# Own places for the first and last row, another lead order on GpSimd and ScalarE, and all eight rows as straight code

## What is computed

```python
h = x + xattn(layernorm(x), ctx, ctx)        # softmax(q k^T / 4) v, then Wo, bo
h1 = einsum('gmh,goh->gmo', layernorm(h), W1) + b1   # g = row, 8 of them, no nonlinearity
out = h + einsum('gmo,gho->gmh', h1, W2) + b2
```

## Time and profile before

| | us |
|---|---|
| median of three runs | 559.8 |
| lowest and highest of them | 554.53, 560.4 |
| the profiled execution | 550.82 |
| its span, first to last instruction | 548.7 |
| PE busy in the span | 529.4 (96%) |
| DVE, ACT, POOL busy | 456.7, 387.0, 278.7 |

### The profile page before, as it was taken

How to read it: one execution, slowest core, us unless ns; L and a number is a source line. 1 busy time by engine, 2 the same in 40 slices (tenths; PEclk the granted TensorE clock), 3 DMA queues, 4 the chain that set the end, 5 groups by cost and what they waited for, 6 DMA issues and landing times.

```text
span 548.7 us, 13740 instructions
## 1 busy us (share of the span) xinstructions
PE 529.4 (96%) x4515; PEld 350.3 (64%) x4515; DVE 456.7 (83%) x841; ACT 387.0 (71%) x704; POOL 278.7 (51%) x320
## 2 busy tenths in 40 slices
PE   8999999999999999999988999999999999989987
PEld 7876674665666667666565666666666667544466
DVE  5896858899989999899877999899889999878234
ACT  7225657877887787777875777776888787667831
POOL 7136417751876159732865149741876156413131
PEclk9986999999999999999998999999999999999999
DMA  7666265535763466555652565544653366130201
GB/s 251 137 161 204 70 182 140 155 89 131 210 162 105 118 186 184 149 146 154 170 157 62 132 184 161 173 111 131 188 159 91 71 184 164 42 78 2 92 9 38
DMA packets 46742, 73.12 MB, mean 133 GB/s; under 512 B 12162, under 2 KB 22730, under 8 KB 46666
## 3 DMA queue, kind: packets, MB, share of 16 engines
q1 hardware_dynamic: 46666, 72.18, 48.0%
HBM read 41.99 MB, written 4.47 MB: 85 GB/s over the span
## 4 chain that ended last, share of the span: by engine, by line
PE 64%; DVE 10%; issue 7%; ACT 6%; SPq 5%; DMA 5%; POOL 3%; DVEq 0%; POOLq 0%; ACTq 0%
PE pv L589 17%; PE st L575 13%; PE nat L564 8%; PE misc L769 7%; PE misc L650 7%; PE misc L640 7%; DVE neg_max L1150 5%; ACT probs L969 4%; SPq L401 3%; ACT normed L1016 2%; DMA qs<-max_hi 2%; DMA x_in<-x 2%; DVE stats L1160 1%; PE st L551 1%; DVE y L1228 1%
## 5 line engine op out<-in xcount | busy, mean ns | idle before, releaser
L969 ACT ACTIVATE probs<-st 128x512 f32<-128x512 f32 x502 | 285.8, 599 | 127.6 <-PE st L575 120.9
L1150 DVE TENSOR_REDUCE neg_max<-nat 128x1 f32<-128x512 f32 x505 | 330.4, 682 | 52.3 <-PE nat L564 48.6
L564 PE MATMUL nat<-ks,qs 63*128 63x512 f32 x505 | 224.9, 468 | 2.5 <-DVE neg_max L1150 1.3
L575 PE MATMUL st<-qs,ks 64*128 64x512 f32 x502 | 217.9, 465 | 7.0 <-issue 2.9
L575 PEld LDWEIGHTS st<-qs,ks 64*128 64x128 f32 x502 | 90.2, 187 | 92.3 <-ACT probs L969 61.8
L589 PE MATMUL pv<-probs,vs 128*32 128x512 f32 x1024 | 133.1, 609 | 1.2 <-ACT probs L969 1.2
L564 PEld LDWEIGHTS nat<-ks,qs 63*128 63x128 f32 x505 | 91.5, 187 | 10.6 <-DVE neg_max L1150 5.3
L769 PE MATMUL misc<-w_in 64*128 64x256 f32 x512 | 74.0, 378 | 0.0
L1391 POOL TENSOR_SCALAR var_eps<-mean_var 128x4 f32<-128x4 f32 x16 | 3.6, 227 | 117.0 <-DVE mean_var L1166 109.4
L769 PEld LDWEIGHTS misc<-w_in 64*128 64x128 f32 x512 | 53.6, 188 | 5.8 <-issue 1.7
L589 PEld LDWEIGHTS pv<-probs,vs 128*32 128x32 f32 x1024 | 22.7, 108 | 45.6 <-issue 34.4
(11 more groups left out here) (223 smaller groups left out, 1049.9 us busy)
## 6 DMA issues: line engine op xcount, KB each, us to landing
ks<-hi SPq DMA_DIRECT2D x64, 128.0 KB, 2.5
qs<-hi SPq DMA_DIRECT2D x64, 128.0 KB, 2.6
w_in<-w SPq DMA_DIRECT2D x16, 512.0 KB
w_in<-w2T SPq DMA_DIRECT2D x16, 512.0 KB
x_in<-x SPq DMA_DIRECT2D x8, 512.0 KB, 4.2
ctx_in<-ctxT SPq DMA_DIRECT2D x8, 512.0 KB, 4.4
ks<-lo SPq DMA_DIRECT2D x32, 128.0 KB, 2.5
qs<-lo SPq DMA_DIRECT2D x32, 128.0 KB, 2.6
```

Of the source, the lines that this page charges most:

```text
L564: mm((nat_of(n) if bank is None else bank)[:, :], qs[own, 2 * g + jj, c * P:(c + 1) * P], ks[own, 2 * g + jj, :], start=True, stop=True).t ...
L575: mm(st_of(u, prep)[:, :], ks[rows(jp), 2 * g + jj, kc * P:(kc + 1) * P], qs[rows(jp), 2 * g + jj, :], start=True, stop=True).then_inc(st_ ...
L969: act.activation(probs[kc % PROBS][:, j, :], st_of(u, prep)[:, :], ACT.Exp).then_inc(exp_done, 1)
L1150: dve.tensor_reduce(neg_max[:, g % 2, at:at + 1], (nat_of(n) if bank is None else bank)[:, :], AX.X, ALU.max, negate=True).then_inc(max_do ...
```

## The change

`turns` becomes a plain loop of the program that writes the kernel, so each engine has eight turns of straight code; `wait_apart` becomes `wait`, and the register values and the `passed` semaphores go. The tables move into a class `Steady` with the values of before, with `First` for row 0 and `Final` for row 7 beside it, which replace some of them; `places(b)` picks one, and steps with places over 64 go by the table of the row that they belong to.

```diff
+            for b in range(B):
+                turn(b, b % 2, b > 0, b < LAST, b < LAST - 1)
-            turn(0, 0, False, True, True)
-            turn(1, 1, True, True, True)
-            with eng.Fori(1, B // 2 - 1) as pair:
-                turn(2 * pair, 0, True, True, True)
-                turn(2 * pair + 1, 1, True, True, True)
-            turn(B - 2, 0, True, True, False)
-            turn(B - 1, 1, True, False, False)
...
+class First(Steady):
+    CHAIN_UNITS = ((0, 0, 0, 0, 0, 0), (3, 3, 5, 6, 6, 7), (9, 9, 9, 9, 10, 10), (10, 11, 11, 11, 11, 11), (13, 13, 13, 13, 13, 14), (17, 17, 17, 26, 31, 32), (32, 33, 34, 35, 35, 35), (37, 37, 38, 38, 38, 39), (41, 42, 42, 42, 43, 43))
+    W21_UNITS = (48, 48, 49, 50, 51, 52, 55, 58, 60, 60, 66, 66, 67, 67, 68, 68)
+    MAXT_UNITS = ((56, 56), (7, 8), (22, 26), (44, 44))
+    PV_UNITS = (4, 10, 15, 22, 24, 33, 36, 40, 44, 45, 47, 54, 57, 61, 62, 64)
+    HI_AT = (9, 9, 11, 15)
+    STATS_AT = (13, 14, 27, 27)
...
+class Final(Steady):
+    CHAIN_UNITS = ((0, 0, 0, 0, 0, 0), (2, 2, 6, 6, 6, 6), (6, 6, 9, 12, 12, 13), (13, 16, 17, 17, 19, 19), (19, 19, 20, 21, 22, 22), (23, 24, 25, 26, 27, 27), (28, 28, 28, 28, 29, 29), (30, 34, 34, 34, 36, 36), (36, 36, 40, 44, 46, 46))
+    YT_UNITS = (37, 37, 37, 37, 37, 37, 37, 37)
+    Z_UNITS = (43, 44, 44, 48, 55, 55, 55, 55)
+    MAXT_UNITS = ((34, 60), (11, 11), (24, 25), (37, 39))
+    PV_UNITS = (8, 13, 15, 17, 30, 31, 34, 36, 39, 46, 50, 53, 58, 61, 65, 66)
+    MASK_AT = (50, 63)
+    MAX_AT = (39, 12, 27, 43)
+    OUT_AT = (61, 62)
...
-FIRST_W21_UNITS = (21, 23, 23, 25, 25, 25, 25, 26, 27, 27, 27, 27, 27, 27, 27, 27)
+FIRST_W21_UNITS = (15, 16, 17, 19, 20, 20, 26, 26, 28, 28, 28, 29, 29, 30, 31, 31)
-FIRST_X_SPLIT_AT = 6
+FIRST_X_SPLIT_AT = 0
+FIRST_WO_AT = 9
-LAST_ST = 44
+LAST_ST = 40
```

SyncE, in turn 0:

```diff
+                if not post:
+                    load_ffn(0, 0)
+                    load_ffn(0, 1)
+                    load_bias(0)
                 if load:
                     load_x(b + 2)
```

```diff
-                    if not post and u < FIRST_WARM:
-                        wait(pe, v_ready, 2)
-                        warm_half(0, WARM_BANKS)
-                        warm_half(1, WARM_BANKS)
```

ScalarE: `ctx_split(1)` moves from unit 1 to just ahead of the turns, `x_split(1)` to unit 0; the activation into `odd_sum` at unit 57 of the last row gets a wait for `even_out`. VectorE: `w_rest(WO)` moves from ahead of the turns into unit 9 of row 0. GpSimd's lead:

```diff
             inverse_root(0, 1)
+            x_norm(1)
+            ctx_rest(1)
             pool.wait_ge(const_in, CONSTS)
-            v_stack(0, 0)
-            v_stack(0, 1)
-            x_norm(1)
-            v_stack(0, 2)
-            v_stack(0, 3)
-            ctx_rest(1)
+            for g in range(QUADS):
+                v_stack(0, g)
             x_rest(1)
```

More of the change, by code:

```diff
@@ L793, in jobs @@
             def jobs(b, odd, u, post, prep, load):
-                for n, at in enumerate(W21_UNITS):
+                here, prior = places(b), places(b - 1)
+                for n, at in enumerate(prior.W21_UNITS):
                     if post and at == UNITS + u:
                         w21_step(b, n, prep)
-                for t, at in enumerate(MAXT_UNITS[1]):
+                for t, at in enumerate(here.MAXT_UNITS[1]):
                     if at == u:
@@ L812, in jobs @@
                         w21_step(0, n, True)
-                for t, at in enumerate(MAXT_UNITS[2]):
+                for t, at in enumerate(here.MAXT_UNITS[2]):
                     if at == u:
@@ L817, in jobs @@
                                 wait(pe, lo_ready, 4 * (b + 1) + 4)
-                            wait_apart(pe, max_done, UNITS * b + 48)
+                            wait(pe, max_done, UNITS * b + 48)
                         maxT_half(b, 2, t)
-                for n, at in enumerate(YT_UNITS):
+                for n, at in enumerate(here.YT_UNITS):
                     if post and at == u:
@@ L826, in jobs @@
                                 wait(pe, v_ready, 2 * (b + 1) + 1)
-                            wait_apart(pe, norm_ready[1], 4 * b)
+                            wait(pe, norm_ready[1], 4 * b)
                         yT_step(b - 1, n)
-                for t, at in enumerate(MAXT_UNITS[3]):
+                for t, at in enumerate(here.MAXT_UNITS[3]):
                     if at == u:
@@ L835, in jobs @@
                                 wait(pe, y_ready, 2 * b - 1)
-                            wait_apart(pe, max_done, UNITS * b + 64)
+                            wait(pe, max_done, UNITS * b + 64)
                         maxT_half(b, 3, t)
-                for n, at in enumerate(Z_UNITS):
+                for n, at in enumerate(here.Z_UNITS):
                     if post and at == u:
@@ L843, in jobs @@
                         z_step(b - 1, 1 - odd, n)
-                for n, at in enumerate(W21_UNITS):
+                for n, at in enumerate(here.W21_UNITS):
                     if prep and at == u:
@@ L848, in jobs @@
                         w21_step(b + 1, n, load)
-                for t, at in enumerate(MAXT_UNITS[0]):
+                for t, at in enumerate(here.MAXT_UNITS[0]):
                     if prep and at == u:
@@ L854, in jobs @@
                                 wait(pe, out_ready, 2 * b)
-                            wait_apart(pe, max_done, UNITS * (b + 1) + 16)
+                            wait(pe, max_done, UNITS * (b + 1) + 16)
                         maxT_half(b + 1, 0, t)
             def turn(b, odd, post, prep, load):
+                here, prior = places(b), places(b - 1)
                 for u in range(UNITS):
@@ L1163, in aggregate @@
                 wait(dve, stat_done[which], 4 * b + 4)
-                wait_apart(dve, rstd_ready[which], b)
+                wait(dve, rstd_ready[which], b)
                 for c in range(C):
@@ L1242, in turn @@
             def turn(b, odd, post, prep, load):
+                here = places(b)
                 for u in range(UNITS):
@@ L1245, in turn @@
                         row_max(row, n)
-                    for c, at in enumerate(STATS_AT):
+                    if not post and u == FIRST_WO_AT:
+                        w_rest(WO)
+                    for c, at in enumerate(here.STATS_AT):
                         if load and at == u:
```

254 lines of the change are left out of this document (133 added, 121 removed).

## The result

| | before, us | after, us |
|---|---|---|
| median of four runs each, on one chip | 557.72 | 537.66 |
| lowest and highest | 554.53, 560.40 | 536.48, 537.96 |
| profiled execution | 550.82 | 537.72 |
| its span | 548.7 | 535.9 |

The ratio is 0.9639, with a 95% interval of 0.9575 to 0.9702. The two profiled executions are only 13.1 apart. So there are two things to read: where the 13.1 lie, and why the medians are a further 7 us apart.

What follows compares the result with a forecast made beforehand. PE was taken to bound a row, at about 60 us. Straight code 6.2, row 0 with the lead 4.0 and the last row 1.5 sum to 11.7 us off 559.8: median 548.1, range 538 to 556.

Steps and rivals of the forecast that it cites:

- I take the savings off the median as they stand: Whole kernel: savings summed against the profiled 550.8 us are subtracted from the timed median 559.8, 9.0 above it.
- straight code: Rows 2 to 5: without the loop's jump back and register instructions, 6.2 us saved, between 4.2 and 7.5.
- the last row: Row 7: new places close PE's holes and pair work better, 1.5 us saved, between -1 and 4.
- half of the rest: Loop rows: besides the jump's 4.86 us, half of the 2.67 by which the other three stretches exceed row 1.
- rival E: Rows 2 to 5: straight code makes PE's fetch late, 4.4 to 4.9 us each, up to 576; chance 0.03.
- The lead: Ahead of row 0: POOL's and ACT's new order readies ctx 8.3 us and xT 7.9 us earlier.
- Row 0's term: Row 0: earlier ctx and xT and a shorter low clock save 4.0 us, with ends 1.0 and 6.1.
- rival D: Row 0: the clock never falls, so the row gives 6.1 us and the median is 546.0; chance 0.05.
- my -1: Last row: pair 0's mask, 0.7 us of ACT, moves from unit 29 to 50, where ACT is busy: -1.
- rival B: Last row: y comes late for the tail, the row loses 3.5 us, median 553.1; chance 0.08.
- Rival C: Whole kernel: only the loop's jump counts and the tables are worth nothing, median 554.9; chance 0.08.
- Rival A: Row 0: the clock stays low through its start, so the row gives 1.0 us, median 551.1; chance 0.14.

Runs made afterwards that it cites:

- repeated run of before: The kernel before, timed and profiled again with no edit: 556.39 us, ratio 1.0035; its profile fell on an execution of 560.66 us.
- the 34 runs: Those of 45 unedited runs of the kernel before, on three chips, that the ratios use: median 557.0 us, 550.80 to 562.03.
- lead-only kernel: Changed kernel with row 0's tables, warm-up pairs and SP's order as before; POOL's and ACT's lead order and W_O's split as changed: 537.35 us, ratio 0.9678.
- second-half kernel: Changed kernel with the last row's places as before up to unit 35, new from unit 36 on, LAST_ST 40: 542.43 us, ratio 0.9755.

## Why the prediction was wrong in size, and what it had right

**The step that failed** is the one that I passed over in a sentence: "I take the savings off the median as they stand". It treats the 9.0 us between the profiled execution and the median as a constant that the change can't touch. The repeated run of before shows what it can be: falls of the clock in the last row, 20.5 us in that execution, which the one profile I had did not contain. That profile's low time was 17.6 us (clock 0.984), where the 34 runs have 28.7; at 0.38 us each that is 4.2 of the 6.2 us between 550.8 and 557.0. The new places take most of that low time away, the last row's above all. By the same slope, as an estimate, the change from 28.7 to 8.3 us is worth 7.8 us of the median's 20.1, and 12.3 are left at equal clock. Forecast were 11.7, of which 3.0 (4.0 less 1.0) stood for a shorter low clock in row 0. I had seen this in the range, with 4 us, and gave it no rival of its own.

By terms, in the medians and taken out one at a time, straight code is worth 7.9 to 8.3 us (taken at 6.2), row 0 and the lead 2.2 (taken at 4.0), and the last row 9.4 (taken at 1.5). That makes 19.5 to 19.9 of the 20.1. The term that was mis-sized by most is the last row's, and its error alone is nearly the whole miss.

**Straight code**, taken at 6.2 between 4.2 and 7.5, gave 7.7 between the profiles, 6.9 when added alone and 7.9 to 8.3 when taken out. The mechanism was right: PE's hole at the jump, 2.9 us, is gone, and the low clock behind it with it. Mis-sized was "half of the rest": the 2.67 us by which the loop's other stretches exceed row 1 was no scatter. With the loop back they are 60.2 to 60.6 again, in straight code 59.5, at full clock both times. The difference between the stretches showed it, and the argument that the register instructions are beside running matmuls was no reason to halve it. That the register instructions are what makes the loop's rows longer is not shown apart from the increments.

**Late fetch in straight code** (rival E) did not come: four rows within 0.03 us of each other. The Trainium skill (Runtime: NRT & Kernel Launch, Instruction fetch mechanics) has straight code fetched ahead in sequence, and this trace agrees.

**The lead** came as worked out: ctx_lo at 37.0 (36.3 forecast), xT_lo at 40.9 (40.6), PE's wait for ctx 0.43 and 0.63 us in the two profiles of the changed kernel and not 1.1. In row 0 the clock was back at 49.72, later than the 48 that I had set as a sign, and in the second profile at 44.83 (44.6 forecast), where the first `odd_sum` stands at 79.45 (79.5 forecast). That last hit is luck in part: I had counted the work up to unit 37, and `First` has the copy behind unit 40. **Row 0's term** of 4.0 was nevertheless too high: 2.2 came. The step that failed in it is the marker. I read the gain at unit 37, by 83.40. Between the profiles the way from the first unit to that copy shrank by 3.5 us (48.8 to 45.4), but the way from there to the second copy grew by 2.2 (24.51 to 26.68), because `First` puts most of the v products behind unit 37. The reading "so it is slow there and not idle" was not enough either: where the clock was full, PE waited for ctx_lo instead and came to the second copy no sooner, so the late ctx was the limit there and not the clock. The lead-only kernel shows that the tables on the whole bring nothing beyond the earlier ctx. (In the sum, a clock that never falls makes 77.9 by its own figures and not 77.3, so rival D was worth 5.5 and not 6.1.)

**The last row**, taken at 1.5 between -1 and 4, gave 5.0 at full clock and 7.9 to 9.4 in the medians, outside its own range by either. I counted PE's idle time in it, and under 1 us for better pairing, as all that could be won, and took 1.5. The idle time did go (2.8 of the 4.25), but PE's busy time fell as well, by 2.1 in the three stretches, and in the medians the clock came on top. The mask in the fuller stretch of ACT, my -1, is not seen: that stretch is 2.3 us shorter.

**y in time** (rival B): forecast with a margin of 1.9, measured with 1.4, so it did not decide. **Rival C**, only the jump, is excluded by 537.66. **Rival A and rival D** stood for the clock in row 0. The changed kernel lies between them, 6.83 us low in one profile and 3.41 in the other, where the forecast had the second. For D I quoted the Trainium skill (TensorE: Matmul & The Clock Gate, Why this matters for your kernels) with idle gaps as what brings the clock down. In the 6.89 us ahead of the fall PE was idle 1.18 in all, less than that rule asks of one gap, and the clock fell; in the last row of before it fell behind a stretch with PE busy 3.67 of 3.96 us. The measurement decides: the absence of long idle gaps was no protection here.

**The warm-up pairs** I dismissed since "the clock did not hold with them". With ctx late it did not; with ctx early it does (low time 1.8 against 8.3 us), and the lead-only kernel, which has the pairs too, has the full clock in its profile up to 88.55 us (it falls there for 3.41 us). They cost nothing that can be seen, and the version with them is the best that was measured, if not by more than the intervals.

Open is which entries of `Final` matter within each half (the four banks from unit 40, z at unit 55, the chain's steps at units 12 and 13). For the second-half kernel, where its falls lie is argued from the repeated run of before and not shown, since its profile has no fall in that row. Why the clock falls in some executions and not in others is open too.

## What to carry to other kernels

Before pricing a change, look at the clock of several executions and not only of the profiled one: where time and mean clock go together over the runs, the gap between profile and median is a term of its own, and an edit to the place where the clock falls can move it. In this kernel such places were the rows with less work than the others, first and last, and spreading what work there is over the last one was worth more than the holes it closed. Read a gain at a marker up to which the two versions have done the same work. An engine that is busy at a low clock ahead of a late input may lose nothing by it: here a full clock only made it wait 1.50 us.

## What the runs showed that I had not expected

- The clock fell behind a stretch that is almost all busy by the profile: 3.67 of 3.96 us, 20 matmuls, nearly all of 64 rows. In four other profiles with the same places it held, so the busy share alone doesn't tell.
- Executions of the kernel before spread by 2% (550.80 to 562.03 among the 34), and go with the mean granted clock: 0.38 us for each us at 1.2 GHz, not the 0.5 that a PE-bound kernel would give.
- The jump back cost 4.42 us on PE's queue in the repeated run and 4.52 before; on SyncE's queue of the same loop the longer of the two branches was 59 ns. The instructions of line 331 in the repeated run of before:

```profile
L331 PEldq COMPARE_BRANCH  x2: 76/2246/4415, 286.0 to 412.5; - x2
...
L331 SPq COMPARE_BRANCH  x2: 48/54/59, 286.4 to 412.9; - x2
```

- A 128-row matmul of 128 columns set between two `st` of 64 rows took 0.42 us of PE's path, as much as a `st`.
